# A two-layer gated attention and expert block: TensorE's visits in the first attention regrouped from two key tiles to three

## What is computed

```
q = ln((x @ Wq + bq) as 16 heads of 16)            # ln over the 16 of a head, with weight and bias
k, v = y_main @ Wk + bk, y_main @ Wv + bv          # k is ln'ed per head too
ctx  = softmax(q k^T / 4) v                        # over 1585 keys
ctx += softmax(q k_dca^T / 4) v_dca                # over the 16 extra keys, own weights
x = x + tanh(g) * (ctx @ Wo + bo)
```

## Time and profile before

| | before |
|---|---|
| median of 3 runs | 2046.72 us (2046.35 to 2048.01) |
| the profiled execution | 2044.75 us |
| its span | 2043.0 us |
| TensorE matmul busy, whole span | 1876.8 us (92%) |
| VectorE busy | 1173.6 us (57%) |
| ScalarE busy | 1037.8 us (51%) |
| mean granted clock of TensorE | 0.963 |
| first S of the attention | 56.64 us |
| last copy of sums | 390.71 us |

### The profile page before, as it was taken

One profiled execution on the slowest core, in us unless ns is written; L12 is line 12 of the kernel. 1 busy time (PEld: TensorE's weight loads), 2 busy tenths in 40 slices (PEclk: granted clock), 3 DMA queues, 4 the chain that ended last, 5 costly groups with the idle time before them and its releaser, 6 DMA issues.

```text
span 2043.0 us, 29167 instructions
## 1 busy us (share of the span) xinstructions
PE 1876.8 (92%) x8775; PEld 1281.9 (63%) x8775; DVE 1173.6 (57%) x1893; ACT 1037.8 (51%) x1703; POOL 321.4 (16%) x292
## 2 busy tenths in 40 slices
PE   5889898859997999999999999999999994999998
PEld 3444444548886666666666666666666663888886
DVE  8565746246666665546654476544665445566665
ACT  2576677613333565556655565555655551222222
POOL 3010101024441100000000000000000002444452
PEclk8899999969998999999999999999999995999999
DMA  2422404064441110000100001000000001255453
GB/s 90 101 59 59 99 19 101 1 215 109 108 114 40 33 33 0 0 0 1 33 0 0 0 1 33 0 0 0 0 1 0 0 0 36 73 116 112 108 115 78
DMA packets 110124, 96.56 MB, mean 47 GB/s; under 512 B 72836, under 2 KB 94472, under 8 KB 109416
## 3 DMA queue, kind: packets, MB, share of 16 engines
q1 hardware_dynamic: 110056, 95.67, 18.8%
HBM read 73.73 MB, written 1.44 MB: 37 GB/s over the span
## 4 chain that ended last, share of the span: by engine, by line
PE 81%; DVE 10%; ACT 2%; SPq 2%; POOL 2%; issue 2%; DMA 1%; ACTq 0%; DVEq 0%; POOLq 0%
PE ps L1137 18%; PE ps L1074 17%; PE ps L390 16%; PE ps L401 8%; PE ps L954 4%; PE ps L941 4%; PE ps L1151 3%; PE ps L1085 2%; PE ps L888 2%; DVE s_rk L1631 2%; SPq L491 2%; POOL s_stage L705 1%; PE ps L1109 1%; PE ps L1146 1%; DVE s_rq L1627 1%
## 5 line engine op out<-in xcount | busy, mean ns | idle before, releaser
L852 ACT ACTIVATE s_p<-ps,s_g,s_rk 128x256 f32<-128x256 f32 (+1 forms) x832 | 416.7, 560 | 298.5 <-PE ps L1074 268.5
L1074 PE MATMUL ps<-s_qq,s_ctxT 128*128 (+2 forms) x1248 | 498.9, 513 | 2.7 <-ACT s_ksq L826 2.7
L1137 PE MATMUL ps<-s_p,s_ctx 128*128 128x512 f32 (+1 forms) x832 | 416.7, 595 | 12.8 <-ACT s_p L852 12.8
L1663 DVE TENSOR_TENSOR s_dsum<-s_dsum,s_p 128x512 f32<-128x512 f32 (+1 forms) x384 | 265.8, 692 | 234.0 <-ACT s_p L852 222.3
L1074 PEld LDWEIGHTS ps<-s_qq,s_ctxT 128*128 128x128 f32 (+1 forms) x1248 | 231.3, 186 | 200.0 <-issue 163.3
L390 PE MATMUL ps<-s_xT,s_wgus 128*128 128x512 f32 x1440 | 350.4, 393 | 3.8 <-DVE s_hw L1559 3.5
L390 PEld LDWEIGHTS ps<-s_xT,s_wgus 128*128 128x128 f32 x1440 | 272.6, 189 | 62.4 <-DVE s_hw L1559 3.9
L770 ACT ACTIVATE s_p<-ps,s_bsm 128x1024 f32<-128x1024 f32 x208 | 219.3, 1110 | 93.1 <-PE ps L954 82.9
L1137 PEld LDWEIGHTS ps<-s_p,s_ctx 128*128 128x128 f32 (+1 forms) x832 | 156.9, 189 | 76.8 <-ACT s_p L852 24.6
L1561 DVE TENSOR_TENSOR s_hs<-s_hw,s_hs 128x512 fp32r<-128x512 f32 x120 | 141.3, 1177 | 82.5 <-ACT s_hs L333 82.5
L401 PE MATMUL ps<-s_hs,s_wds 128*128 128x512 f32 x720 | 183.9, 391 | 1.8 <-DVE s_hs L1561 1.8
(11 more groups left out here) (240 smaller groups left out, 1837.2 us busy)
## 6 DMA issues: line engine op xcount, KB each, us to landing
s_wB<-w1s SPq DMA_DIRECT2D x64, 256.0 KB, 3.9
s_kT<-s_kst SPq DMA_DIRECT2D x96, 128.0 KB, 2.3
s_kT<-s_kst SPq DMA_DIRECT2D x96, 80.0 KB, 2.1
s_wB<-w0s SPq DMA_DIRECT2D x16, 384.0 KB, 3.7
s_wB<-w0s SPq DMA_DIRECT2D x16, 256.0 KB, 4.1
s_wgu<-in_L_ffn_Wg_dram SPq DMA_DIRECT2D x64, 64.0 KB, 2.8
s_wgu<-in_L_ffn_Wu_dram SPq DMA_DIRECT2D x64, 64.0 KB, 2.6
s_wd<-in_L_ffn_Wd_dram SPq DMA_DIRECT2D x64, 64.0 KB, 2.5
```

Of the source, the lines that this page charges most:

```text
L852: ins = nc.scalar.activation(p1[0:r, BANK1[t], j, :], ps[0:r, BANK1[t], j * SQ:(j + 1) * SQ], ACT.Exp, bias=g1[0:r, 3:4], scale=rk_col(t, ...
L1074: ins = nc.tensor.matmul(out, lhs(x_), rhs(y_), start=first and n == 0, stop=last and n == 2)
L1137: nc.tensor.matmul(ps[:, 4, :], ctx1[0:ROWS1[t], t, :], p1[0:ROWS1[t], BANK1[t], :, :].rearrange("p a n -> p (a n)"), start=t == 0, stop=t ...
L1663: v.tensor_tensor(dsum[0:r, :], dsum[0:r, :], pt[0:r, :], ALU.add).then_inc(s.summed, 1)
```

## The change

Visits hold three tiles, and four at the end of a group: 4 visits in a group where there were 6. The list of preparation steps is now by step, not by visit, and each stands directly behind the S issued at that step, so that a visit may hold up to three. All but one of them keep the step at which they stood; the last key chunk of the next batch goes from step 47 to 48. Buffers, banks and the other engines' lists stay as they are.

```diff
--- before.py
+++ after.py
@@ -115,23 +115,23 @@
 STEPS0 = NG * KT
 
 
-VISITS = [(KT * g + 2 * j, 3 if j == 5 else 2) for g in range(NG) for j in range(6)]
+VISITS = [(KT * g + 3 * j, 4 if j == 3 else 3) for g in range(NG) for j in range(4)]
 COPIES = 3
 
 
-def visit_work(b, v):
+def step_work(b, step):
 
     more = b + 1 < B
-    first = {0: ("keys", b, 1, 0), 1: ("keys", b, 1, 1), 2: ("keys", b, 1, 2), 3: ("keys", b, 1, 3)}
-    second = {2: ("query", b, 1), 7: ("sums", b, 0), 8: ("query", b, 2), 13: ("sums", b, 1), 14: ("query", b, 3),
-              19: ("sums", b, 2)}
+    work = {0: ("keys", b, 1, 0), 2: ("keys", b, 1, 1), 4: ("keys", b, 1, 2), 5: ("query", b, 1), 6: ("keys", b, 1, 3),
+            16: ("sums", b, 0), 18: ("query", b, 2), 29: ("sums", b, 1), 31: ("query", b, 3), 42: ("sums", b, 2)}
     if b:
-        second[0] = ("sums", b - 1, NG - 1)
+        work[1] = ("sums", b - 1, NG - 1)
     if more:
-        first.update({4 + t: ("proj", b + 1, t) for t in range(KT)})
-        first.update({20: ("keys", b + 1, 0, 0), 21: ("query", b + 1, 0), 22: ("keys", b + 1, 0, 3)})
-        second.update({20: ("keys", b + 1, 0, 1), 21: ("keys", b + 1, 0, 2)})
-    return first.get(v), second.get(v)
+        for t, at_step in enumerate((8, 10, 13, 15, 17, 19, 21, 23, 26, 28, 30, 32, 34)):
+            work[at_step] = ("proj", b + 1, t)
+        work.update({43: ("keys", b + 1, 0, 0), 44: ("keys", b + 1, 0, 1), 45: ("query", b + 1, 0),
+                     46: ("keys", b + 1, 0, 2), 48: ("keys", b + 1, 0, 3)})
+    return work.get(step)
 
 
 SQUARE = (18, 27, 35, 37)
@@ -142,8 +142,7 @@
 
     order = [("proj", 0, t) for t in range(KT)] + [("keys", 0, 0, c) for c in range(4)] + [("query", 0, 0)]
     for b in range(B):
-        for v in range(len(VISITS)):
-            order += [w for w in visit_work(b, v) if w]
+        order += [step_work(b, step) for step in range(STEPS0) if step_work(b, step)]
     order.append(("sums", B - 1, NG - 1))
     return {w: n for n, w in enumerate(order)}
 
@@ -984,15 +983,10 @@
             for n in range(3):
                 scores_at(n)
             for b in range(B):
-                for v, (step, tiles) in enumerate(VISITS):
-                    n = b * STEPS0 + step
-                    first, second = visit_work(b, v)
-                    scores_at(n + 3)
-                    prepare(first)
-                    scores_at(n + 4)
-                    prepare(second)
-                    if tiles == 3:
-                        scores_at(n + 5)
+                for step, tiles in VISITS:
+                    for k in range(tiles):
+                        scores_at(b * STEPS0 + step + k + 3)
+                        prepare(step_work(b, step + k))
                     for k in range(tiles):
                         values(b, step + k)
             turn_sums(B - 1, NG - 1)
```

## The result

| | before | after |
|---|---|---|
| median | 2046.53 us (4 runs) | 2071.7 us (2067.24 to 2073.18, 4 runs) |
| ratio to before | | 1.0096 (95%: 1.0071 to 1.0121) |
| profiled execution, its span | 2044.75, 2043.0 us | 2071.4, 2069.7 us |
| first to last copy of the sums | 309.78 us | 332.72 us |
| TensorE's mean granted clock | 0.963 | 0.960 |

The kernel became about 25 us slower, forecast 2071. A second measurement beside another experiment gave 2072.37 us and 1.0099 (1.0078 to 1.0121).

The account below looks back on a forecast made before the run. TensorE and ScalarE, tied through buffers and level in the plain stretch, were taken to bound the first attention. Last batch +8.0 and three batches with projections +16.8 sum to +24.8: 2069.6 us profiled, 2071 forecast, range 2056 to 2085.

Parts of the forecast that it names:

- one exponential covers it, none does: With four probability buffers, one exponential covers a visit of three's wait (0.51 us lost), none a visit of four's.
- third-place query: Last batch, two groups: a query transposition behind a visit's last S adds 0.56 less 0.09 us, giving 17.35 a group.
- The last batch: Last batch, nothing to prepare in most visits: +8.0 us, as +1.3 first group, +2.4, +2.4, +1.9; bounds 0 and 12.
- The way: From an exponential's end through last S and V to the next exponential's buffer: 0.80 plus 0.77, together 1.57 us.
- The batches with projections: Three batches where TensorE is the slower engine: 5.6 us a batch, +16.8 in all; bounds a batch -2.7 to +9.
- saved turns: 24 visits a batch become 16: 32 removed, each giving 0.34 us at most, 10.9 us where TensorE alone sets the pace.
- key steps bunched, two visits with a third-place step, one of four: First group of each batch with projections: bunched key steps and longer visits cost +1.0 us.
- rival 3: Idle drops TensorE's clock to 1.2 GHz at each visit of four, adding 22 us: 2093; chance 0.08.
- The ties: S(n) waits for exp(n-3) through score banks; exp(n) waits for V(n-4) through the four probability buffers.
- The root: Fourth group: S(44) waits for exp(41), behind a root with table loads; 2.02 us idle becomes some 3.5; group +1.8.
- Rival 1: Turns saved and waits hidden: 32 x 0.34 us comes back, giving 2036 us; chance 0.04.
- the rule on drains: Between V and S: changing tiling mode drains TensorE, two drains a visit; by this alone the change would save 10.9 us.

Follow-up runs that it names:

- e1: The changed kernel with six probability buffers instead of four: 2048.65 us, 0.9995 of the kernel before.
- e5: The changed kernel with five probability buffers instead of four: 2053.91 us, 1.0008 of the kernel before.
- e6: The kernel before, its visits untouched, with three probability buffers in use instead of four: 2070.83 us, 1.0090 of the kernel before.
- e7: The changed kernel with the new visits in the last batch alone, old visits in the other batches: 2058.97 us, 1.0032 of the kernel before.
- e9: The changed kernel with the first two projections of each next batch one step later (8 to 9, 10 to 11): 2068.91 us, 1.0075 of the kernel before.
- e4: The changed kernel with a group as visits of 3,3,3,2,2 tiles instead of 3,3,3,4: 2059.46 us, 1.0048 of the kernel before.
- e8: The kernel of e1 (six buffers) with visits of 2,4,2,2,3 tiles: 2047.94 us, 0.9984 of the kernel before.
- e10: The changed kernel as it is, measured again beside e9 on the same chip: 2072.37 us, 1.0099 of the kernel before.

## Why the prediction was right

**The mechanism.** The step that carried it, "one exponential covers it, none does", is shown from both sides: buffers added under the new visits take the loss away (e1, e5), a buffer removed under the old ones makes it (e6), with the same holes. The third-place query cost 0.44 to 0.46 (0.94 against 0.48), forecast 0.47. One of the prediction's own signs failed: TensorE's idle time for exponentials was to reach 25 us or more and came to 19.2. One was missed narrowly: the last batch's groups were to stand 17 to 17.5 us apart, and the two full ones stand 16.9. The others held: the longest such wait was 3.41 us, three times, and TensorE's waits for bank 7, summed from its timeline from 85 us to the last copy, went from 21.6 to 25.1 us.

**The last batch.** Forecast +8.0, measured 69.78 - 62.00 = +7.8. Behind it two terms were off and cancelled, which is luck: the first group is +2.6 (forecast 1.3), the other three +5.2 (6.7). The way was priced at 1.57 us and is 1.48, seen bare behind a visit of four. An exponential was priced at 1.06 and comes every 1.0 in a row without holes (four take 4.13, three 3.12); the row of six that gave 1.06 must hold small waits. Together these are the difference between 17.35 and 16.87. Of the first group's +2.6, 1.3 is the slow first V (2.79 us for 1.50), a clock term that the forecast did not have there. Where that V was fast, in e7 and e9, the last batch lost 6.2 and 6.0 us.

**The batches with projections.** For the second: 

| group | forecast | measured |
|---|---|---|
| first | +1.0 | +2.8 |
| second | +0.6 | +0.3 |
| third | +2.2 | +1.7 |
| fourth | +1.8 | +1.6 |
| sum | 5.6 | 6.4 |

From first to last copy the four batches make 332.72 - 309.78 = 22.9. The first group of the first batch ended 83.43 - 80.93 = 2.5 later, some of it the DMAs; that is 25.4 together, forecast 24.8. In the second group the saved turns nearly paid for the waits, as worked out: "22.2; with restarts up to 23.0" became 22.0.

The mis-sized term is the first group's, "key steps bunched, two visits with a third-place step, one of four". I had not walked it by visits. The projection at step 8 stands third, behind the last key chunk, whose reading by VectorE waits in turn for the 3.5 us on the query. TensorE stood idle 1.20 us there, and the next V ran at the lower clock and lost 2.77 - 1.50 = 1.3 us more. The wait belongs to the place of the step. The lower clock need not: in e4 the same wait left V at 1.50. This is a part of rival 3, in the first groups and not at the visits of four, where it had been put: all visits of four kept V at 2.37.

So the whole came out closer than its parts. The ties and the way carry most of the loss, as said. But e9, which keeps every visit and buffer of the changed kernel, has a stretch only 325.15 - 309.78 = 15.4 us longer than before, and the other 7.6 us to the changed kernel's 22.9 lie nearly all in the first groups' waits and clock.

**The root.** The idle time of 2.02 us was to become some 3.5; it is 3.41, with the lower clock behind it as before:

```profile
229.81 1.22 PE L940 MATMUL ps<-s_qz,s_kT 96*128 96x512 f32 x2 [3.41 <-ACT s_p L769]
230.96 2.79 PE L953 MATMUL ps<-s_p,s_vg 128*32 128x256 f32 x24
```

**Rival 1 and the rule on drains.** The gain is real, 0.34 us a turn in e1's rows, so the Trainium skill's sentence that a change of the tiling mode drains TensorE (TensorEngine Tiling (Array Packing), section Tiling Modes) and the trace agree in kind, though no run here tells a drain from other costs of a turn. It could not reach the end: with four buffers V's tie ate it, with six the fourth score pair's wait did (e1). In e8, with one turn fewer, 0.2 us a group is left of it.

## What to carry to other kernels

When an in-order engine works in visits on a ring of buffers, count for each visit size how much of the other engine's work is left between the last operand it must wait for and the first buffer it gives back: ring size less tiles in the visit. Each tile more in the visit takes one operation of cover away, and once it is gone the round trip (here 1.48 us) shows in full; to save 0.34 us of turn is no match for it. Before enlarging visits, enlarge the ring, and then look at the next ring: here six buffers only brought the time back to that of before. Idle time that ends at a semaphore of another engine may be reserve (82.9 us here, of which a larger ring freed 2): take its length as a limit only where the waiting engine is otherwise back to back.

## What the runs showed of the hardware that was not expected

TensorE's granted clock fell to its lower level, 1.2 GHz, after only 1.20 us of idle, behind scores and a transposition (the row at 169.22), in the same place of two batches: V took 2.77 and 2.33 us there instead of 1.50. In e4, e5 and e1 the idle at the same place of the second batch was 1.20, 1.44 and 1.46 us, and V took 1.50 each time. In the kernel before, 1.58 us of idle at 141.18 had left the next V at 1.07. So the length of one idle piece did not decide. And where the fall comes is not fixed by the code at that point alone: in e9 the V before the root ran slow (4.05 us), in the changed kernel the V behind it (2.79), with no edit near either, and the first V of the last batch was slow in both profiled executions of the changed kernel (2.79 and 2.78 us) but not in e7 or e9. What made the clock fall in each of these places is open.

The part behind the attention differs between profiled executions too: from the last copy to the end of the span it took 1652.3 us in the kernel before, 1653.6 in the changed one, 1658.0 in e10 and 1661.5 in e9, with the same instructions. That scatter is as wide as the smaller effects here, so they were read by the stretch. Between the profiled executions of e10 and e9 it takes back 3.5 of the stretch's 7.8 us. Whether it also explains that the medians differ by only 3.5 us isn't shown.
